# Reordering TensorE's step in a pipelined local-attention layer

## Chip, cores and metric

The kernel runs on one core of a Trainium2 chip. The metric is the device time of one launch in microseconds, lower is better. Before the change three runs gave 4150.61, 4144.84 and 4150.33 us, median 4150.33 us. A separate profiled execution took 4145.04 us.

## What is computed

The input is x, 8 sequences of 512 tokens with 128 features. Stage 1 is a causal attention with 16 heads of 8, which the change does not touch. Its output u goes through six layers of stage 2:

```
for each of 6 layers:
    xs = shift_tokens(u)                    # half of the features one token late
    q, k, v = xs @ Wqkv                     # 16 heads of 64
    q, k = rotary(l2norm(q)), rotary(l2norm(k))
    out = local_attention(q, k, v)          # windows of 32, each sees itself and the one before
    u = u + out @ Wo
    u = u + W2(a * gelu(gate)),  a, gate = W1(layernorm(shift_tokens(u)))
output = (stage 1's result) + u
```

## The kernel before, in words

Everything is laid out features by tokens. `build_stage2` (L594 on) writes one program for each engine, and the engines meet only through semaphores. Each engine executes its own list strictly in the order of the code; `wait_ge` holds the engine's queue at that place.

**The step.** A layer's attention is cut into 64 steps: 8 sequences (s) of 8 steps (p), a step being four heads of half a sequence (256 tokens). `step_no` numbers them through the program as n. The work of one step is spread over six consecutive iterations of the loop `steps` (L682), by the lags of L578: in iteration n an engine does projection and values of step n, the sum of squares and rotation of n-1 (`LAG_MIX`), the normalised queries and keys of n-2 (`LAG_NORM`), the scores of n-3 (`LAG_SCORE`), the transposes and value products of n-4 (`LAG_VALUE`) and the output projection of n-5 (`LAG_WO`). After the eighth sequence, iterations with s = 8 empty the pipeline while the feed-forward part starts. In iterations p = 6 and 7 of each sequence but the first, a layer-norm mean or variance of the previous sequence is added.

**TensorE's order in an iteration** (L1164 on):
- the mask (L1188): two bf16 products of an identity with the band, 128x256 each, put 1e30 into both score banks where a key isn't allowed; it waits for `norm_done` (queries and keys of that step written) and `exp_done` (banks read)
- the scores (L1198): 128 products of 32x32 tiles; then four transposes of the probabilities (L1178) into `tr_bank`; then mean or variance (L1150, L1154) where there is one
- the projection (L1221 to L1223): twelve fp32r products of 256 columns into `proj_ps`; it waits for `prod_done` (both rotary products of the last step have read that bank)
- the values (L1233 to L1235): three products of 512 columns into `tr_bank`, the bank that the transposes used; they wait for `pt_first` and `pt_second`, that is, until ScalarE (L907) and VectorE (L1062) have copied the transposed probabilities out
- the output projection (L1246 to L1249), six products; the value products (L1269), 32 tiles; the sums of squares (L1287).

**VectorE's order** (L1034 on): least score of both halves (L1043, `least`), copy of the transposes (L1062), `y_rest` (L1070), `centre` (L1014) at p = 6, `write_qk` (L792, two instructions that multiply `rotated` by `inv_norm`, both in SBUF), at p = 0 `divide` (L1019) and `scale_shift` (L1025), two reciprocals (L1050), at p = 4 the residual (L1092), then the cosine product (L1102) and the sine product (L1107), which read `proj_ps`.

**GpSimd's order** (L808 on): addition of the squares (L837); then, behind `prod_done`, both rotations (`rotate`, L814, SBUF only); at p = 3 the rest of the next tokens (L827); both normalisations of the probabilities (L823).

**ScalarE's order** (L893 on): at p = 3 the next tokens (L925), copy of the transposes (L907), eight exponentials (L917), the layer norm's part (L881, L886), square of the projection (L946), copy of the values out of `tr_bank` (L950), `y_high` (L958), logarithm (L967) and exponential (L973) of the sums.

SyncE's queue loads weights and tokens and moves each values tile into its shifted place (L750, L751) once `v_done` says that it is written.

## Time and profile before

| | |
|---|---|
| median of three runs | 4150.33 us |
| profiled execution | 4145.04 us |
| its span, first to last instruction | 4143.2 us |
| mean granted TensorE clock | 0.985 of full speed |
| PE busy | 3880.8 us, 94% |
| DVE busy, ACT busy, POOL busy | 76%, 76%, 61% |

PE is TensorE's matmuls and PEld its weight loads, DVE is VectorE, ACT is ScalarE, POOL is GpSimd and SP is SyncE. A row of a group gives line, engine, operation, output and inputs, shape, count, then busy time and mean ns of one, then the idle time in front of it and what ended it. A row of a timeline gives the start in us, the time in us, engine, line and operation, and merged neighbours have a count behind x. Matmuls overlap, and their ends are modelled, so the distance between two starts is what a piece of TensorE work costs.

### The profile page before, as it was taken

The page shows a single profiled execution, that of the slowest core. Times are in us where ns is not written, and L with a number is a line of the kernel's source. Part 1 is how long each engine was busy: PE and PEld are TensorE (multiplying, and loading weights), DVE is VectorE, ACT ScalarE, POOL GpSimd, SP SyncE. Part 2 cuts the span into 40 slices and gives each one's busy share as a digit, 9 for nine tenths or more (in the row PEclk, how much of TensorE's full clock was granted, in tenths as well). Part 3 has the DMA queues.
Part 4 walks back from the last instruction along what each step waited for, and adds up shares of the span by engine and source line. Part 5 has one row for each costly group of instructions (what it writes and reads, how often), then busy time and mean ns, then how long its engine had stood idle before and what let it go on. Part 6 is the DMA issues. An engine that isn't in the chain of part 4 may idle for free.

```text
span 4143.2 us, 192715 instructions
## 1 busy us (share of the span) xinstructions
PE 3880.8 (94%) x79584; PEld 3037.8 (73%) x79584; DVE 3144.8 (76%) x5678; ACT 3146.7 (76%) x10376; POOL 2543.9 (61%) x2584
## 2 busy tenths in 40 slices
PE   6888886999999999989999999999899999999998
PEld 3555554888866888848888668888488886688884
DVE  6778874888866888848888668888488886688884
ACT  5777775888865888848888658888388886588883
POOL 4766665766645666637666456666276664566660
PEclk9999998999999999999999999999999999999999
DMA  1000001111111111111111111111111111111110
GB/s 35 2 2 2 2 2 51 44 50 44 47 59 39 44 50 47 42 51 44 50 47 45 58 37 47 48 46 44 51 44 50 45 47 58 36 48 45 50 44 24
DMA packets 100984, 167.64 MB, mean 40 GB/s; under 512 B 26224, under 2 KB 33648, under 8 KB 99824
## 3 DMA queue, kind: packets, MB, share of 16 engines
q1 hardware_dynamic: 100080, 154.89, 12.7%
q8 instruction: 653, 10.70, 1.1%
q14 instruction: 251, 2.06, 0.2%
HBM read 26.13 MB, written 2.10 MB: 7 GB/s over the span
## 4 chain that ended last, share of the span: by engine, by line
PE 72%; issue 7%; POOL 3%; DVE 1%; ACT 0%; DMA 0%; SPq 0%; POOLq 0%; DVEq 0%; ACTq 0%
PE s_bank L1198 13%; PE s_bank L1269 10%; PE s_bank L1287 9%; PE s_bank L1178 6%; PE s_proj L1221 4%; PE s_proj L1222 4%; PE s_proj L1223 4%; PE s_bank L1246 2%; PE s_bank L1248 2%; PE s_bank L1249 2%; PE s_bank L1235 2%; PE s_bank L1234 2%; PE s_bank L1233 2%; PE s_bank L1188 2%; PE s_bank L1160 2%
## 5 line engine op out<-in xcount | busy, mean ns | idle before, releaser
L814 POOL TENSOR_TENSOR s_rotated<-s_rotated,s_by_sin 128x512 f32<-128x512 f32 x768 | 976.7, 1293 | 308.8 <-DVE s_by_sin L1107 308.7
L917 ACT ACTIVATE s_probs<-s_bank,s_neg_max 128x64 f32<-128x64 f32 x3072 | 900.3, 309 | 5.7 <-DVE s_neg_max L1043 5.7
L823 POOL TENSOR_TENSOR s_probs<-s_probs,s_rden 128x256 f32<-128x256 f32 x768 | 454.8, 613 | 651.1 <-DVE s_rden L1050 651.1
L1102 DVE TENSOR_TENSOR s_rotated<-s_proj,s_cos 128x1024 f32<-128x1024 f32 x384 | 469.1, 1222 | 268.1 <-ACT s_sq L946 262.6
L917 ACT ACTIVATION_READ_ACCUMULATOR s_probs<-s_bank,s_neg_max 128x1 f32 x3072 | 632.6, 206 | 0.0
L1198 PE MATMUL s_bank<-s_qk 32*32 32x64 f32 x49152 | 597.1, 224 | 10.3 <-issue 9.6
L1198 PEld LDWEIGHTS s_bank<-s_qk 32*32 32x32 f32 x49152 | 530.0, 103 | 96.8 <-issue 96.0
L792 DVE SCALAR_TENSOR_TENSOR s_qk<-s_inv_norm,s_rotated 128x512 f32<-128x512 f32 x768 | 573.5, 787 | 4.7 <-ACT s_inv_norm L973 4.5
L1221 PE MATMUL s_proj<-s_xs_high,s_w_high 128*128 128x256 f32 x1536 | 495.4, 323 | 66.6 <-POOL s_xs_rest L827 30.6
L213 POOL TENSOR_TENSOR s_probs<-s_probs,s_rden 128x384 f32<-128x384 f32 (+3 forms) x512 | 406.4, 802 | 207.6 <-DVE s_rden L406 203.8
L837 POOL TENSOR_TENSOR s_sq<-s_sq 128x512 f32<-128x512 f32 x384 | 491.8, 1281 | 59.6 <-ACT s_sq L946 59.6
L907 ACT ACTIVATE s_probs_t<-s_bank 64x512 f32<-64x512 f32 x384 | 227.1, 591 | 358.3 <-PE s_bank L1178 358.1
L1107 DVE TENSOR_TENSOR s_by_sin<-s_proj,s_sin 128x1024 f32<-128x1024 f32 x384 | 466.4, 1214 | 0.0
L946 ACT ACTIVATE s_sq<-s_proj 128x1024 f32<-128x1024 f32 x384 | 396.7, 1033 | 73.3 <-PE s_proj L1223 73.3
L1269 PE MATMUL s_bank<-s_probs_t,s_v 128*64 128x64 f32 x12288 | 451.0, 228 | 0.0
L1223 PE MATMUL s_proj<-s_xs_high,s_w_rest 128*128 128x256 f32 x1536 | 436.7, 284 | 0.0
L1222 PE MATMUL s_proj<-s_xs_rest,s_w_high 128*128 128x256 f32 x1536 | 436.1, 284 | 0.0
L1287 PE MATMUL s_bank<-s_sq,s_same_head 128*128 128x256 f32 x1536 | 435.4, 406 | 0.0
L1269 PEld LDWEIGHTS s_bank<-s_probs_t,s_v 128*64 128x64 f32 x12288 | 397.5, 140 | 51.7 <-issue 4.2
L1043 DVE TENSOR_REDUCE s_neg_max<-s_bank 128x4 f32<-128x256 f32 x768 | 291.6, 420 | 189.1 <-PE s_bank L1198 188.4
L1221 PEld LDWEIGHTS s_proj<-s_xs_high,s_w_high 128*128 128x128 f32 x1536 | 293.1, 191 | 99.9 <-issue 36.8
L295 ACT ACTIVATE s_probs<-s_bank,s_neg_max 128x384 f32<-128x384 f32 (+3 forms) x512 | 271.8, 533 | 89.4 <-DVE s_neg_max L397 85.8
(123 smaller groups left out, 8648.0 us busy)
## 6 DMA issues: line engine op xcount, KB each, us to landing
s_v<-s_v SPq DMA_DIRECT2D x384, 192.0 KB
s_v<-s_v SPq DMA_DIRECT2D x384, 64.0 KB
s_qk<-f_wqk SPq DMA_DIRECT2D x6, 1024.0 KB, 5.5
s_xs_raw<-u SPq DMA_DIRECT2D x48, 128.0 KB, 2.5
s_xf<-u SPq DMA_DIRECT2D x48, 128.0 KB, 2.4
s_xs_raw<-u SPq DMA_DIRECT2D x48, 127.8 KB, 2.8
s_xf<-u SPq DMA_DIRECT2D x48, 127.8 KB, 3.2
s_qk<-f_wv SPq DMA_DIRECT2D x6, 512.0 KB, 6.2
```

What stands on the lines that cost most here:

```text
L792: last = nc.vector.scalar_tensor_tensor(qk[:, quad % 2, i, :, at:at + TOKS], by, NORM_CUT, rotated[:, par, i, :, :], ALU.min, ALU.mult)
L814: nc.gpsimd.tensor_tensor(rotated[:, par, :, half, :], rotated[:, par, :, half, :], by_sin[:, :, 1 - half, :], (ALU.subtract, ALU.add)[half])\
L837: nc.gpsimd.tensor_tensor(own[:, :, 0, :], own[:, :, 0, :], own[:, :, 1, :], ALU.add)\
L917: last = nc.scalar.activation(probs[:, par, h, b, :], score_bank[h][:, b * KEYS:(b + 1) * KEYS], ACT.Exp, scale=-1.0, bias=neg_max[:, par, ...
L1102: nc.vector.tensor_tensor(rotated[:, par, :, :, :], proj_ps[:, :, :, :], rot_cos[:, :, :, toks], ALU.mult).then_inc(S["prod_done"], 1)
L1107: nc.vector.tensor_tensor(by_sin[:, :, :, :], proj_ps[:, :, :, :], rot_sin[:, :, :, toks], ALU.mult).then_inc(S["prod_done"], 1)
L1198: last = nc.tensor.matmul(score_bank[e][to:to + WIN, w * KEYS:(w + 1) * KEYS], qk[rows, quad % 2, 0, c, WIN + at:WIN + at + WIN], qk[rows, ...
L1221: nc.tensor.matmul(proj_ps[:, i, c, :], w[0], xs_high[:, s % 2, at:at + TOKS], start=True, stop=False)
L1222: nc.tensor.matmul(proj_ps[:, i, c, :], w[0], xs_rest[:, s % 2, at:at + TOKS], start=False, stop=False)
L1223: last = nc.tensor.matmul(proj_ps[:, i, c, :], w[1], xs_high[:, s % 2, at:at + TOKS], start=False, stop=True)
L1269: last = nc.tensor.matmul(mixed[HD * h:HD * (h + 1), pair, t, :, e, :], v[:, cols, (half * NT + t) * 2 + e, at:at + HD], probs_t[:, e, t, ...
L1287: last = nc.tensor.matmul(ss_bank[:, i * TOKS:(i + 1) * TOKS], same_head[:, :], sq[:, place(p, LAG_MIX)[2], i, 0, :], start=True, stop=True)
```

## The change

The work itself stays the same; the order on four engines, one buffer and one type change.

- TensorE, iteration n: scores (their mask is already in place), transposes, mean or variance, **output projection**, **values**, value products, sums, **projection**, **mask of the next iteration's scores**.
- The mask's operands are fp32r in place of bf16 ("rounded").
- VectorE: the second `least` goes behind the copy of the transposes. The two rotary products move to the next iteration (lag 1 in place of 0) and stand in front of `write_qk`. `y_rest` moves an iteration earlier, behind the reciprocals. `divide` and `scale_shift` go to the end.
- GpSimd: addition of squares, rest of the tokens, `rotate(0)`, both normalisations, `rotate(1)`.
- ScalarE: the values' copy and the layer norm's part go between the two halves of the exponentials; the square goes between logarithm and exponential.
- `sq` has one buffer in place of two.

```diff
@@ gpsimd
                     pool.wait_ge(S["sq_done"], m + 1)
-                    own = sq[:, place(p, LAG_MIX)[2], :, :, :]
-                    nc.gpsimd.tensor_tensor(own[:, :, 0, :], own[:, :, 0, :], own[:, :, 1, :], ALU.add)\
+                    nc.gpsimd.tensor_tensor(sq[:, :, 0, :], sq[:, :, 0, :], sq[:, :, 1, :], ALU.add)\
                       .then_inc(S["sqadd_done"], 1)
-                    pool.wait_ge(S["prod_done"], 2 * m + 2)
-                    rotate(0)
-                    rotate(1)
                 if p == XS_STEP and s < NSEQ - 1:
                     tokens_rest(s + 1)
+                if live(s, p, LAG_MIX, first):
+                    pool.wait_ge(S["prod_done"], 2 * (n - LAG_MIX) + 2)
+                    rotate(0)
                 if live(s, p, LAG_SCORE, first):
                     normalise(0)
                     normalise(1)
+                if live(s, p, LAG_MIX, first):
+                    rotate(1)
@@ scalar
                     exponentials(0)
-                if live(s, p, LAG_SCORE, first):
-                    exponentials(1)
+                if full:
+                    act.wait_ge(S["v_mm"], n + 1)
+                    nc.scalar.activation(v[:, p // TILES, 2 * (p % TILES), :], tr_bank[:, :], ACT.Copy)\
+                      .then_inc(S["v_done"], 1)
...
+                if live(s, p, LAG_SCORE, first):
+                    exponentials(1)
...
+                if full:
+                    act.wait_ge(S["proj_done"], n + 1)
+                    if not (first and p == 0):
+                        act.wait_ge(S["ss_done"], n)
+                    nc.scalar.activation(sq[:, :, :, :], proj_ps[:, :, :, :], ACT.Square)\
+                      .then_inc(S["sq_done"], 1)
@@ vector
                     least(0)
-                    least(1)
...
+                if score:
+                    least(1)
                 if ln and p == LN_STEP + 1:
                     centre(l * NSEQ + s - 1)
+                if live(s, p, LAG_MIX, first):
+
+                    m = n - LAG_MIX
+                    _, half, par = place(p, LAG_MIX)
+                    toks = slice(half * TOKS, (half + 1) * TOKS)
+                    dve.wait_ge(S["sq_done"], m + 1)
...
+                    nc.vector.tensor_tensor(rotated[:, par, :, :, :], proj_ps[:, :, :, :], rot_cos[:, :, :, toks],
+                                            ALU.mult).then_inc(S["prod_done"], 1)
...
+                    nc.vector.tensor_tensor(by_sin[:, :, :, :], proj_ps[:, :, :, :], rot_sin[:, :, :, toks],
+                                            ALU.mult).then_inc(S["prod_done"], 1)
                 if norm:
                     m = n - LAG_NORM
                     dve.wait_ge(S["inv_done"], m + 1)
...
                     write_qk(p).then_inc(S["norm_done"], 1)
@@ tensor
-                    pe.wait_ge(S["norm_done"], m + 1)
...
-                        nc.tensor.matmul(score_bank[e][:, 0:NW * KEYS], ident_b[:, :], band_b[:, 1 if half or e else 0, :],
-                                         start=True, stop=False, skip_group_check=True)
...
+                if full:
+                    if p == 0:
+                        pe.wait_ge(S["xs_rest"], l * NSEQ + s + 1)
+                    if live(s, p, LAG_VALUE, first):
+                        pe.wait_ge(S["pt_first"], n - LAG_VALUE + 1)
+                        pe.wait_ge(S["pt_second"], n - LAG_VALUE + 1)
...
...
+                if full:
+                    if not (first and p == 0):
+                        pe.wait_ge(S["prod_done"], 2 * n)
...
+                if live(s, p, LAG_SCORE - 1, first):
+
+                    half = place(p, LAG_SCORE - 1)[1]
+                    pe.wait_ge(S["norm_done"], n + 1 - LAG_SCORE + 1)
...
+                    for e in range(2):
+                        nc.tensor.matmul(score_bank[e][:, 0:NW * KEYS], ident_r[:, :], band_r[:, 1 if half or e else 0, :],
+                                         start=True, stop=False, skip_group_check=True)
```

## Rows read from the trace of the kernel before

**Rows 1.** The page's busy times of the engines.

```profile
PE 3880.8 (94%) x79584; PEld 3037.8 (73%) x79584; DVE 3144.8 (76%) x5678; ACT 3146.7 (76%) x10376; POOL 2543.9 (61%) x2584
```

**Rows 2.** Timeline of one iteration without layer norm, TensorE alone, first row of each part.

```profile
1529.03 0.65 PE L1178 MATMUL s_bank<-s_ident,s_probs 128*128 128x128 f32 x4
1529.43 0.37 PE L1221 MATMUL s_proj<-s_xs_high,s_w_high 128*128 128x256 f32 x1
...
1530.96 0.40 PE L1233 MATMUL s_bank<-s_w_high,s_xs_high 128*128 128x512 f32 x1
...
1531.66 0.28 PE L1246 MATMUL s_bank<-s_y_high,s_w_high 128*128 128x256 f32 x1
...
1532.46 1.15 PE L1269 MATMUL s_bank<-s_probs_t,s_v 128*64 128x64 f32 x32
...
1533.55 1.13 PE L1287 MATMUL s_bank<-s_sq,s_same_head 128*128 128x256 f32 x4
...
1534.51 0.38 PE L1188 MATMUL s_bank<-s_band_b,s_ident_b 128*128 128x256 bf16 x2
...
1534.82 1.56 PE L1198 MATMUL s_bank<-s_qk 32*32 32x64 f32 x128
...
1536.38 0.65 PE L1178 MATMUL s_bank<-s_ident,s_probs 128*128 128x128 f32 x4
```

**Rows 3.** The same iteration, VectorE and GpSimd.

```profile
1529.79 0.69 DVE L1062 COPY s_probs_t<-s_bank 64x512 f32<-64x512 f32 x1
...
1531.12 1.28 DVE L792 SCALAR_TENSOR_TENSOR s_qk<-s_inv_norm,s_rotated 128x512 f32<-128x512 f32 x2
...
1533.64 1.22 DVE L1102 TENSOR_TENSOR s_rotated<-s_proj,s_cos 128x1024 f32<-128x1024 f32 x1 [0.73 <-ACT s_sq L946]
...
1534.78 1.21 DVE L1107 TENSOR_TENSOR s_by_sin<-s_proj,s_sin 128x1024 f32<-128x1024 f32 x1
...
1536.08 2.52 POOL L814 TENSOR_TENSOR s_rotated<-s_rotated,s_by_sin 128x512 f32<-128x512 f32 x2 [1.09 <-DVE s_by_sin L1107]
1536.35 0.76 DVE L1043 TENSOR_REDUCE s_neg_max<-s_bank 128x4 f32<-128x256 f32 x2 [0.36 <-PE s_bank L1198]
```

**Rows 4.** Timelines, VectorE and GpSimd: first iterations of a layer; a p = 3.

```profile
3002.21 1.21 DVE L1107 TENSOR_TENSOR s_by_sin<-s_proj,s_sin 128x1024 f32<-128x1024 f32 x1
3003.34 2.38 DVE L792 SCALAR_TENSOR_TENSOR s_qk<-s_inv_norm,s_rotated 128x512 f32<-128x512 f32 x2
...
3003.50 3.35 POOL L814 TENSOR_TENSOR s_rotated<-s_rotated,s_by_sin 128x512 f32<-128x512 f32 x2 [1.12 <-DVE s_by_sin L1107]
...
849.84 2.45 DVE L792 SCALAR_TENSOR_TENSOR s_qk<-s_inv_norm,s_rotated 128x512 f32<-128x512 f32 x2
849.92 1.82 POOL L827 TENSOR_TENSOR s_xs_rest<-s_xs_raw,s_xs_high 128x544 fp32r<-128x544 f32 x1
```

**Rows 5.** Timeline of an iteration whose mask waited for `write_qk`.

```profile
3009.22 3.01 DVE L792 SCALAR_TENSOR_TENSOR s_qk<-s_inv_norm,s_rotated 128x512 f32<-128x512 f32 x2
...
3012.61 1.57 PE L1198 MATMUL s_bank<-s_qk 32*32 32x64 f32 x128
```

**Rows 6.** Groups of instructions: two weight loads and the centring.

```profile
L1221 PEld LDWEIGHTS s_proj<-s_xs_high,s_w_high 128*128 128x128 f32 x1536 | 293.1, 191 | 99.9 <-issue 36.8 <-POOL s_xs_rest L827 31.4 <-DVE s_by_sin L1107 31.0
...
L1188 PEld LDWEIGHTS s_bank<-s_band_b,s_ident_b 128*128 128x128 bf16 x768 | 73.8, 98 | 64.2 <-DVE s_qk L792 8.3 <-issue 3.4
...
L1014 DVE TENSOR_TENSOR s_xc<-s_xf,s_bank 128x512 f32<-128x512 f32 x48 | 32.6, 679 | 0.6
```

**Rows 7.** Timeline, the transposes that begin p = 0 of two sequences.

```profile
1514.32 0.65 PE L1178 MATMUL s_bank<-s_ident,s_probs 128*128 128x128 f32 x4
...
1574.77 0.65 PE L1178 MATMUL s_bank<-s_ident,s_probs 128*128 128x128 f32 x4
```

**Rows 8.** Stretches: us, busy times, PEclk (granted clock), DMA share, GB/s.

```profile
1849.00:1853.00 4.00, 3.69 (x15) 3.10 (x15) 0.00 (x0) 1.02 (x1) 0.00 (x0) 0.58 0.35 119
...
1771.00:1777.00 6.00, 4.13 (x170) 3.52 (x170) 2.50 (x6) 3.02 (x19) 1.06 (x2) 0.99 0.01 3
```

More of the change, by code:

```diff
@@ L625, in build_stage2 @@
         ident = sb("s2_ident", [P, P])
-        ident_b = sb("s2_ident_b", [P, P], BF16)
-        band_b = sb("s2_band_b", [P, 2, NW * KEYS], BF16)
+        ident_r = sb("s2_ident_r", [P, P], F32R)
+        band_r = sb("s2_band_r", [P, 2, NW * KEYS], F32R)
         same_head = sb("s2_same_head", [P, P])
@@ L639, in build_stage2 @@
         v = sb("s2_v", [P, 2, VTILES, INNER // 2])
-        sq = sb("s2_sq", [P, 2, 2, 2, TOKS])
+        sq = sb("s2_sq", [P, 2, 2, TOKS])
         by_sin = sb("s2_by_sin", [P, 2, 2, TOKS])
@@ L940, in step @@
                     log_var(f)
-                if full:
-                    act.wait_ge(S["proj_done"], n + 1)
-                    if not (first and p < 2):
-                        act.wait_ge(S["ss_done"], n - 1)
-                    nc.scalar.activation(sq[:, place(p, 0)[2], :, :, :], proj_ps[:, :, :, :], ACT.Square)\
-                      .then_inc(S["sq_done"], 1)
-                    act.wait_ge(S["v_mm"], n + 1)
-                    nc.scalar.activation(v[:, p // TILES, 2 * (p % TILES), :], tr_bank[:, :], ACT.Copy)\
-                      .then_inc(S["v_done"], 1)
+                if live(s, p, LAG_SCORE, first):
+                    exponentials(1)
                 if live(s, p, LAG_VALUE, first):
@@ L1081, in step @@
                     write_qk(p).then_inc(S["norm_done"], 1)
-                if not first and s > 1 and p == 0:
-                    divide(l, s - 2)
-                    scale_shift(l, s - 2)
                 if score:
@@ L1087, in step @@
                     inverse_sum(1)
+                if live(s, p, LAG_VALUE, first):
+                    m, par = n - LAG_VALUE, place(p, LAG_VALUE)[2]
+                    dve.wait_ge(S["y_done"], m + 1)
+                    if not (first and p == LAG_VALUE):
+                        dve.wait_ge(S["wo_done"], m)
+                    nc.vector.tensor_tensor(y_rest[:, :, :], y_bank[:, :].rearrange("p (a t) -> p a t", a=2),
+                                            y_high[:, par, :, :].bitcast(F32), ALU.subtract).then_inc(S["y_rest"], 1)
                 if not first and p == WO_STEP - 1:
@@ L1093, in step @@
                       .then_inc(S["attn_res"], 1)
-                if full:
-                    _, half, par = place(p, 0)
-                    toks = slice(half * TOKS, (half + 1) * TOKS)
-                    dve.wait_ge(S["sq_done"], n + 1)
-                    if not (first and p < 2):
-                        dve.wait_ge(S["norm_done"], n - 1)
-                    nc.vector.tensor_tensor(rotated[:, par, :, :, :], proj_ps[:, :, :, :], rot_cos[:, :, :, toks],
-                                            ALU.mult).then_inc(S["prod_done"], 1)
-                    if not (first and p == 0):
-                        dve.wait_ge(S["add_done"], 2 * n)
-                    nc.vector.tensor_tensor(by_sin[:, :, :, :], proj_ps[:, :, :, :], rot_sin[:, :, :, toks],
-                                            ALU.mult).then_inc(S["prod_done"], 1)
+                if not first and s > 1 and p == 0:
+                    divide(l, s - 2)
+                    scale_shift(l, s - 2)
             def ffn_add(f, s):
@@ L1183, in step @@
                     quad, half, par = place(p, LAG_SCORE)
-                    pe.wait_ge(S["norm_done"], m + 1)
-                    if not (first and p == LAG_SCORE):
-                        pe.wait_ge(S["exp_done"], 2 * m)
-                    for e in range(2):
-                        nc.tensor.matmul(score_bank[e][:, 0:NW * KEYS], ident_b[:, :], band_b[:, 1 if half or e else 0, :],
-                                         start=True, stop=False, skip_group_check=True)
                     for w in range(NW):
```

63 lines of the change are left out of this document (27 added, 36 removed).

## The prediction, made before the change was run

> **What bounds the kernel now.** I began with the page's busy times: PE is at 94% of the span, DVE, ACT and POOL at 76, 76 and 61% [rows 1]. A busy PE need not be a full one, so I then took the timeline of one iteration without layer norm and read distances between starts [rows 2]: transposes 0.40 us, projection 1.53, values 0.70, output projection 0.80, value products 1.09, sums 0.96, mask 0.31, scores 1.56. They add up to 7.35 us, the distance between the two transposes, 1529.03 and 1536.38. There is no hole: TensorE is the bound, and every wait of its queue has been met in time. Eight iterations from p = 0 take 1574.77 - 1514.32 = 60.45 us [rows 7], that is 1.65 more than 8 x 7.35: 0.82 for the mean and 0.82 for the variance. On the other engines [rows 3] the reader should see the cover that the order gives: between transposes and values lies the projection (1.53 us), under which the copies run; and `write_qk` (1.28 us for its two instructions) runs while GpSimd rests, its rotations having come long before.
>
> **TensorE's own work.** Nothing is added or left out, so the sum stays 7.35. The mask turns fp32r: its weight load takes 191 ns in place of 98 [rows 6], and it is now met behind a wait, where nothing hides it. Bounds: 0 (loaded ahead) and 0.09 us; its columns cost what the projection's do, about 0.12 us for 256 in both forms (1.53/12, and half of the mask's 0.31 less a change of tiles) [rows 2]. I take 0.05 us. The new wait stands in front of the scores, which is why it counts.
>
> **The values' wait.** Let T be the first transpose. Values must wait for both copies. VectorE's starts at T + 0.76 (1529.79 - 1529.03), just when the transposes are done, and takes 0.69: it ends at T + 1.45 [rows 2, 3]. TensorE now has only the six output products beside it: at the projection's pace of 0.12 us they end at T + 0.40 + 0.72 = T + 1.12. To TensorE's next product goes at least 0.05 and, with the load, some 0.20 us: values start at about T + 1.65 and 0.53 us of TensorE is lost. From there the queue runs 0.79 + 1.09 + 0.96 + 1.53, to a finished projection at T + 6.02, then mask 0.31 and scores 1.56: by TensorE's order alone an iteration would take 7.89 us.
>
> **VectorE's chain, which I expect to decide.** In the new order VectorE does between T and the mask: copy until T + 1.45, second `least` (0.76 for both, about 0.42 alone) until T + 1.90, cosine product, whose successor starts 1.14 later (T + 3.04), sine product, then `write_qk` [rows 3]. Everything is FIFO, and behind the mask's wait on `norm_done` stand the scores, behind these the transposes, behind these the copy: a closed loop with no slack. The inputs are ready: the square ends some 1.4 us before the next T. `write_qk` now starts right behind the sine product, 1.13 us after that began (T + 4.17), and in the same moment the sine product releases `rotate(0)` on GpSimd. That collision is in the trace of before, where a layer begins: sine product 3002.21, `write_qk` 3003.34, rotation 3003.50, and the two instructions take 2.38 us in place of 1.28 [rows 4]. With a single GpSimd instruction beside it, at 849.84, 2.45 us [rows 4]. So 2.38, ending at T + 6.55. From the end of `write_qk` to the first score go 0.38 us (3009.22 + 3.01 = 3012.23 to 3012.61) [rows 5], with the fp32r load 0.43. Scores start at T + 6.98, the next transposes 1.56 later: **8.55 us an iteration**, 1.20 more than now. The values' wait lies inside this loop and is not added; TensorE, done with the projection at T + 6.02, waits some 0.6 us more at the mask.
> The Trainium skill (SBUF — State Buffer, section Who interferes with whom) says that a VectorE instruction with two SBUF inputs and a GpSimd instruction that reads SBUF exclude each other for their whole length, the later one blocked. By that rule the pair would take its own 1.28 us plus a whole rotation, which by the rows is about 1.26 (half of 2.52): 2.54 us, an iteration of 8.71 us and some 4640 us in all. The row's 2.38 decides for me; that one of the two is blocked and not merely slowed fits it.
>
> **Iterations that differ.** p = 6: `centre` (0.68 us [rows 6]) joins the chain: 9.25. p = 7: the logarithm of the variance now stands behind the copy of the values, and the sums wait for it. Values start at T + 0.40 + 0.82 + 0.72 = 1.94, are in the bank at about 2.9, copy and logarithm (0.6 and 0.7, as every ScalarE pass over 512 columns) end at 4.2; sums at 4.35, so projection, mask, scores at 0.96 + 1.53 + 0.31 + 1.56 later: 8.7. p = 0: `divide` and `scale_shift` (about 1.4 us) now end VectorE's list, meet the normalisations on GpSimd, and push the next first `least`; VectorE has about 1 us spare. Cost at p = 1 between 0 and 1.1 us; I take 0.5. The residual at p = 4 (0.7 us) fits into the same spare time. SyncE's moves of the values start earlier within an iteration and are needed an iteration or more later: nothing. GpSimd: `rotate(1)` and the addition of squares end before T + 3, needed at T + 3.0 and later: nothing while a loop takes over 7 us. One buffer of `sq`: the square waits for the sums just done: nothing.
> A sequence: 8 x 8.55 + 0.7 (p = 6) + 0.15 (p = 7) + 0.5 (p = 1) = 69.75 us against 60.45 [rows 7], 9.3 more. With 7 such sequences in 6 layers: 42 x 9.3 = 391. A layer's first sequence has 5 iterations from the first score on, 1.2 each: 6 x 6 = 36. At a layer's start the values come first (0.70 us [rows 2], twice that at half clock), but the sums no longer stand behind the next values: 0. At its end the feed-forward product waits behind the mask, +1.5, and an emptier iteration follows, -0.5: 6 us. **Sum +433 us**: 4145 + 433 = 4578 for the profiled execution, whose own time is 5 us below the median of the runs; I say 4580.
>
> **Rivals.**
> 1. *No collision* (GpSimd's rotation comes late, or the pair keeps 1.28 us). Then VectorE's loop is 7.45, below the 7.89 of TensorE's order with the values' wait, which decides: (6 x 0.54 + about 0.5 + 0.6) = 4.3 us a sequence, 42 x 4.3 + 30 x 0.54 = 197, so about **4340 us**. For it: in an ordinary iteration of before no pair is slow [rows 3]. Against it: rotation and pair are now released by the same instruction. 7%.
> 2. *Faster*. The one place is the values' wait: if the copies are done before T + 1.12 (0.33 us sooner than the row says, because the first `least` no longer has the second between it and the copy), and the mask never waits, what remains is the projection's slow first product, 1.53 - 12 x 0.12 = 0.09 us an iteration, won 366 times: 4145 - 33 = **4110 us**. Against it: ScalarE, whose queue was empty, took its copy up no sooner than VectorE, so the transposes set that start. 4%.
> 3. *The clock*. TensorE now idles over 1 us an iteration. A stretch in which it was busy only 4.13 of 6 us kept 0.99 of the clock, while one that followed a long idle time had 0.58 [rows 8]. If some windows drop to 1.2 GHz, scores, mask and transposes (2.3 us of the loop) double there: one iteration in five would add 366 x 0.2 x 2.3 = 168, **4750 us**. 5%.
> 4. *The change doesn't do what it says*: the "rounded" mask falls back to a slower form of product. Sums of squares in plain f32 take 0.24 us for 256 columns (0.96/4) [rows 2], twice the 0.12; 2 x 0.12 x 366 = 88, **4670 us**. 3%.
>
> **How the numbers follow.** My forecast has 81%: both of its parts, the loop and the slow pair, stand in rows. Its unknowns are the pair (2.38 to 2.54), the load (0 to 0.09), the p = 1 delay (0 to 1.1) and gaps I have taken as zero or counted twice (0.15 us either way, 366 times, 55 us): 4490 to 4680. To that I add a little on both sides: 4470 to 4700, which also takes in rival 4; rivals 1, 2 and 3 lie outside, 16%. Faster by over 0.2% (about what a measurement can tell from no change): rival 2 alone, 4%. Within 0.2%: 1%. Slower: 95%.
>
> **What the changed kernel's profile would show.** The mean of `write_qk` (L792's successor) goes from 0.7 to about 1.2 us, its second instruction near 1.7; the mask waits for VectorE's `s_qk` in nearly all of 366 iterations, 0.5 to 0.9 us each; the values wait for the copy L1062 by about 0.5 us; T to T is 8.5 to 8.7; PE busy falls to about 85%; DVE idles only between `y_rest` and the first `least`. I am wrong if the pair stays at 1.28 us, if ScalarE or GpSimd is what TensorE waits for, if rotation and pair don't overlap, or if T to T stays under 8.

## The result, and where the profile shows it

The changed kernel took **4502.5 us** (median of 4 runs, 4497.7 to 4507.2) against 4147.6 us for the kernel before on the same chip: a ratio of 1.086 [1.084, 1.088], slower. The forecast was 4580 us in a range from 4470 to 4700; it was right in direction and range and 78 us too high. The profiled execution had a span of 4501.2 us at a mean clock of 0.99, 358 us above the span of before.

The page of the changed kernel: busy times, the chain that ended last by engine, and three groups (busy and mean ns of one, idle before and its releaser).

```profile
PE 4008.9 (89%) x79584; PEld 3062.6 (68%) x79584; DVE 3414.0 (76%) x5678; ACT 3155.0 (70%) x10376; POOL 2692.3 (60%) x2584
...
DVE 36%; PE 31%; issue 13%; POOL 2%; ACT 1%; DVEq 1%; DMA 0%; SPq 0%; POOLq 0%; ACTq 0%
...
L813 POOL TENSOR_TENSOR s_rotated<-s_rotated,s_by_sin 128x512 f32<-128x512 f32 x768 | 1135.8, 1480 | 878.2 <-DVE s_by_sin L1076 878.2
...
L791 DVE SCALAR_TENSOR_TENSOR s_qk<-s_inv_norm,s_rotated 128x512 f32<-128x512 f32 x768 | 906.5, 1221 | 0.0
...
L1286 PE MATMUL s_bank<-s_band_r,s_ident_r 128*128 128x256 f32 x768 | 188.9, 328 | 170.7 <-DVE s_qk L791 163.7
```

Two of these rows for the kernel before, the chain and the group of `write_qk`:

```profile
PE 72%; issue 7%; POOL 3%; DVE 1%; ACT 0%; DMA 0%; SPq 0%; POOLq 0%; DVEq 0%; ACTq 0%
...
L792 DVE SCALAR_TENSOR_TENSOR s_qk<-s_inv_norm,s_rotated 128x512 f32<-128x512 f32 x768 | 573.5, 787 | 4.7 <-ACT s_inv_norm L973 4.5
```

VectorE's busy time has grown by 269 us for the same 5678 instructions [rows 1], and the chain that ends last now runs through VectorE for 36% of the span, where TensorE had 72% of it. The group that grew most is `write_qk` (now L791), by 333 us: 1221 ns in the mean where it had been 787. TensorE's share of busy time fell from 94 to 89% although its instructions are the same in number, and its mask now finds `s_qk` late. The waits of the changed kernel (engine, line, waited for: us in total, times, longest us):

```profile
POOL s_rotated L813 <- DVE s_by_sin L1076: 878.2, 384, 3.5
...
PEld s_bank L1286 <- DVE s_qk L791: 239.5, 334, 2.9
...
PE s_bank L1286 <- DVE s_qk L791: 163.7, 321, 2.5
...
PEld s_bank L1224 <- ACT s_probs_t L907: 91.1, 228, 1.0
...
PE s_bank L1224 <- ACT s_probs_t L907: 52.7, 228, 0.8
...
PE s_bank L1263 <- ACT s_rstd L886: 11.6, 42, 0.3
```

The two waits that the order was expected to create are both there: the mask for `write_qk` (0.5 us each time) and the values for the copies (0.2 us each time). For the values the page names ScalarE's copy L907 as the releaser; VectorE's ends within some 0.1 us of it. The last row is the sums of squares waiting for the logarithm of the variance, and its 42 cases are the 42 iterations with p = 7. One ordinary iteration shows the loop. Timeline, start and length in us, idle time before in brackets; T, its first transpose, is 1622.44.

```profile
1622.44 0.65 PE L1173 MATMUL s_bank<-s_ident,s_probs 128*128 128x128 f32 x4
...
1623.19 0.69 DVE L1057 COPY s_probs_t<-s_bank 64x512 f32<-64x512 f32 x1 [0.36 <-PE s_bank L1173]
...
1623.92 0.42 DVE L1039 TENSOR_REDUCE s_neg_max<-s_bank 128x4 f32<-128x256 f32 x1
...
1623.99 0.47 PE L1224 MATMUL s_bank<-s_w_high,s_xs_high 128*128 128x512 f32 x1 [0.20 <-ACT s_probs_t L907]
...
1624.26 1.21 DVE L1072 TENSOR_TENSOR s_rotated<-s_proj,s_cos 128x1024 f32<-128x1024 f32 x1
...
1625.39 1.21 DVE L1076 TENSOR_TENSOR s_by_sin<-s_proj,s_sin 128x1024 f32<-128x1024 f32 x1
...
1626.52 2.38 DVE L791 SCALAR_TENSOR_TENSOR s_qk<-s_inv_norm,s_rotated 128x512 f32<-128x512 f32 x2
...
1626.68 1.67 POOL L813 TENSOR_TENSOR s_rotated<-s_rotated,s_by_sin 128x512 f32<-128x512 f32 x1 [2.40 <-DVE s_by_sin L1076]
...
1628.96 0.50 PE L1286 MATMUL s_bank<-s_band_r,s_ident_r 128*128 128x256 f32 x2 [0.47 <-DVE s_qk L791]
...
1629.39 1.48 PE L1187 MATMUL s_bank<-s_qk 32*32 32x64 f32 x128
...
1630.86 0.65 PE L1173 MATMUL s_bank<-s_ident,s_probs 128*128 128x128 f32 x4
```

The reader is to follow VectorE without a gap from the copy to 1628.90, then TensorE: mask, scores, and the transposes that release the next copy. That ring closes in 1630.86 - 1622.44 = 8.42 us, where before it was TensorE's own queue that took 7.35 [rows 2]. `write_qk` and the rotation start 0.16 us apart and take 2.38 us together, the very figure of [rows 4].

A second reading places the 358 us to within 1. For every p the distance from one iteration's first transpose to the next is taken in the trace, and its median over the 42 full sequences stands here (us; the last row is another kernel, described below):

```
kernel            p=0   p=1   p=2   p=3   p=4   p=5   p=6   p=7
before            7.34  7.32  7.34  7.33  7.32  7.32  8.11  8.11
after             8.53  8.43  8.43  8.44  8.43  8.43  9.03  8.48
rotation late     7.97  7.69  7.72  7.73  7.74  7.72  8.15  8.47
```

The rows of before and after differ by 8.01 us in a sequence, 336 us in 42. The six first sequences of a layer add 4.8 us each (29). The five stretches between the layers, 114 to 119 us in either kernel, are 7 us shorter in sum than before (577.5 for 584.6), and what follows the last layer's sequences 1 us. That makes 336 + 29 - 8 = 357 us.

### The profile page after: what moved, and what is told of

The parts are those of the page before. It is cut to its first block, busy times and chain, and to the rows that moved or that the text cites. A ratio compares the mean times of both kernels' runs of the same rounds, so it can differ in the third digit from the quotient of the medians.

```text
span 4501.2 us, 192781 instructions
## 1 busy us (share of the span) xinstructions
PE 4008.9 (89%) x79584; PEld 3062.6 (68%) x79584; DVE 3414.0 (76%) x5678; ACT 3155.0 (70%) x10376; POOL 2692.3 (60%) x2584
## 4 chain that ended last, share of the span: by engine, by line
DVE 36%; PE 31%; issue 13%; POOL 2%; ACT 1%; DVEq 1%; DMA 0%; SPq 0%; POOLq 0%; ACTq 0%
DVE s_qk L791 15%; PE s_bank L1187 12%; DVE s_rotated L1072 8%; DVE s_by_sin L1076 8%; PE s_bank L1173 6%; PE s_bank L1286 4%; DVE s_neg_max L1039 3%; PE s_bank L1155 1%; PE s_bank L1263 1%; DVE s_probs_t L1057 1%; PE s_bank L1310 1%; PE s_proj L1155 1%; PE s_bank L1149 1%; ACT s_rstd L886 1%; PE s_proj L1274 1%
## 5 line engine op out<-in xcount | busy, mean ns | idle before, releaser
L813 POOL TENSOR_TENSOR s_rotated<-s_rotated,s_by_sin 128x512 f32<-128x512 f32 x768 | 1135.8, 1480 | 878.2 <-DVE s_by_sin L1076 878.2
L917 ACT ACTIVATE s_probs<-s_bank,s_neg_max 128x64 f32<-128x64 f32 x3072 | 909.4, 311 | 2.7 <-DVE s_neg_max L1039 2.7
L791 DVE SCALAR_TENSOR_TENSOR s_qk<-s_inv_norm,s_rotated 128x512 f32<-128x512 f32 x768 | 906.5, 1221 | 0.0
L822 POOL TENSOR_TENSOR s_probs<-s_probs,s_rden 128x256 f32<-128x256 f32 x768 | 473.9, 637 | 326.5 <-DVE s_rden L1046 326.1
L1039 DVE TENSOR_REDUCE s_neg_max<-s_bank 128x4 f32<-128x256 f32 x768 | 325.1, 424 | 436.9 <-PE s_bank L1187 424.9
L907 ACT ACTIVATE s_probs_t<-s_bank 64x512 f32<-64x512 f32 x384 | 227.2, 592 | 534.8 <-PE s_bank L1173 534.8
L1187 PE MATMUL s_bank<-s_qk 32*32 32x64 f32 x49152 | 573.9, 224 | 7.4 <-issue 7.4
L1187 PEld LDWEIGHTS s_bank<-s_qk 32*32 32x32 f32 x49152 | 509.2, 103 | 67.2 <-issue 15.7
L1057 DVE COPY s_probs_t<-s_bank 64x512 f32<-64x512 f32 x384 | 266.8, 695 | 149.3 <-PE s_bank L1173 149.3
L1286 PE MATMUL s_bank<-s_band_r,s_ident_r 128*128 128x256 f32 x768 | 188.9, 328 | 170.7 <-DVE s_qk L791 163.7
```

The costliest lines, as they stand in the source:

```text
L791: last = nc.vector.scalar_tensor_tensor(qk[:, quad % 2, i, :, at:at + TOKS], by, NORM_CUT, rotated[:, par, i, :, :], ALU.min, ALU.mult)
L813: nc.gpsimd.tensor_tensor(rotated[:, par, :, half, :], rotated[:, par, :, half, :], by_sin[:, :, 1 - half, :], (ALU.subtract, ALU.add)[half])\
L822: nc.gpsimd.tensor_tensor(part, part, by, ALU.mult).then_inc(S["probs_done"], 1)
L917: last = nc.scalar.activation(probs[:, par, h, b, :], score_bank[h][:, b * KEYS:(b + 1) * KEYS], ACT.Exp, scale=-1.0, bias=neg_max[:, par, ...
L1039: nc.vector.tensor_reduce(neg_max[:, par, h, :], score_bank[h][:, 0:NW * KEYS].rearrange("p (b k) -> p b k", k=KEYS), AX, ALU.min).then_in ...
L1187: last = nc.tensor.matmul(score_bank[e][to:to + WIN, w * KEYS:(w + 1) * KEYS], qk[rows, quad % 2, 0, c, WIN + at:WIN + at + WIN], qk[rows, ...
```

## The experiments

Ratios are to the kernel before, run on the same chip in turn, with 95% intervals. "Iteration" is the median distance above, for p from 1 to 5.

### One suspected cost at a time, on the changed kernel

**The rotation taken off the pair.** GpSimd normalises first and rotates after.

```diff
-                if live(s, p, LAG_MIX, first):
-                    pool.wait_ge(S["prod_done"], 2 * (n - LAG_MIX) + 2)
-                    rotate(0)
                 if live(s, p, LAG_SCORE, first):
                     normalise(0)
                     normalise(1)
                 if live(s, p, LAG_MIX, first):
+                    pool.wait_ge(S["prod_done"], 2 * (n - LAG_MIX) + 2)
+                    rotate(0)
                     rotate(1)
```

> The changed kernel with GpSimd's first rotation behind both normalisations, so that it cannot run beside write_qk; nothing is left out. My theory (a closed loop through VectorE, 1.1 us of it the collision of write_qk with the rotation): the pair of write_qk goes from 2.38 to 1.28 us, the mask stops waiting, and an iteration falls from 8.42 to about 7.7 us, where TensorE's order with the values' wait and the projection's wait for the sine product are level. 366 x 0.72 = 264 us less than 4502: about 4240 us. Rival A (the slow pair is hidden, the values' wait alone costs the time): no change, 4490 to 4510. Rival B (only a later GpSimd matters, its normalisations now come sooner): the pair shortens but the iteration stays over 8.2.

Measured: 4283.6 us, 1.0355 [1.0338, 1.0373]. Its timeline, one iteration:

```profile
1626.78 1.22 DVE L1075 TENSOR_TENSOR s_by_sin<-s_proj,s_sin 128x1024 f32<-128x1024 f32 x1
...
1627.91 1.29 DVE L791 SCALAR_TENSOR_TENSOR s_qk<-s_inv_norm,s_rotated 128x512 f32<-128x512 f32 x2
...
1629.37 1.19 POOL L822 TENSOR_TENSOR s_probs<-s_probs,s_rden 128x256 f32<-128x256 f32 x2 [3.62 <-DVE s_rden L1045]
...
1629.72 0.39 PE L1285 MATMUL s_bank<-s_band_r,s_ident_r 128*128 128x256 f32 x2
...
1630.51 2.51 POOL L813 TENSOR_TENSOR s_rotated<-s_rotated,s_by_sin 128x512 f32<-128x512 f32 x2
```

The pair is back at 1.29 us and ends at 1629.20, half a microsecond ahead of a mask that now stands behind the projection without a wait. Three lines moved on GpSimd give back 219 us of the 358 (208 by the two ratios): the collision is the larger part of the loss. The time came out some 40 us above my figure, mostly because I had counted the gain for all 366 iterations: p = 7 gained 0.01 us (8.48 to 8.47; that alone is 30 us) and p = 0 only 0.56. The bound of p = 7 is another. Its sums wait for the logarithm of the variance in all 42 cases of this kind, in the changed kernel and in the one with both edits below, and it keeps 8.47 to 8.49 us whatever is taken from VectorE.

**VectorE's chain shortened elsewhere.** The second `least` goes back in front of the copy; the collision stays.

```diff
                 if score:
                     least(0)
+                    least(1)
                 if live(s, p, LAG_VALUE, first):
...
-                if score:
-                    least(1)
```

> The changed kernel with the second least score back in front of the copy of the transposes, where VectorE has 0.36 us to spare before the transposes are done; nothing else. If VectorE's loop (copy, least, cosine, sine, write_qk, mask, scores, transposes) sets the pace, every iteration loses the 0.38 us that this instruction holds between the copy and the cosine product: 8.42 to 8.05 us, 366 x 0.38 = 139 us, about 4363 us. If the values' wait or ScalarE's order sets it: no change, since the copy ends at the same time; 4495 to 4510.

Measured: 4403.8 us, 1.0646 [1.0628, 1.0663]; iteration 8.10 (expected 8.05), pair unchanged. TensorE has the same work and the same waits in front, so 0.33 us an iteration that appear when VectorE has one instruction fewer between the transposes and the mask show that the ring through VectorE sets the time. Again the iterations with layer norm gained less (p = 7: none), and the whole came 41 us above the figure.

**Both together.** The two edits above in one kernel.

> Both of the two: rotation behind the normalisations and the second least score in front of the copy. VectorE's loop would be near 7.0 us and the one through the projection near 7.3; what is left is TensorE's own order with the values' wait, about 7.6 us. So with the values' wait real: 4502 - 366 x 0.8 = about 4210 us, only 30 us under the run with the rotation alone, and TensorE's mask waits for nothing. If the values' wait cost nothing: iteration 7.3, about 4095 us, under the kernel before.

Measured: 4282.7 us, 1.035 [1.0332, 1.0367]; iteration 7.70 to 7.79, no shorter than that of the rotation alone. Taking 0.33 us more from VectorE bought nothing, so VectorE no longer decides. What does stands in the timeline of this kernel:

```profile
1630.88 0.65 PE L1171 MATMUL s_bank<-s_ident,s_probs 128*128 128x128 f32 x4
...
1631.95 0.28 PE L1210 MATMUL s_bank<-s_y_high,s_w_rest 128*128 128x256 f32 x1
...
1632.43 0.47 PE L1222 MATMUL s_bank<-s_w_high,s_xs_high 128*128 128x512 f32 x1 [0.21 <-ACT s_probs_t L906]
...
1635.16 0.47 PE L1272 MATMUL s_proj<-s_xs_high,s_w_high 128*128 128x256 f32 x1
```

The values start at T + 1.55 and everything behind them follows closely. The pace of the output products (0.12 us) would have let them start at 1632.07: about 0.36 us of TensorE is lost at that wait, and 7.32 + 0.36 = 7.68 is the iteration seen.

**The wait made longer.** To the kernel with both edits: the values stand in front of the output projection, directly behind the transposes.

```diff
+                if full:
...
+                    nc.tensor.matmul(tr_bank[:, :], xs_rest[:, s % 2, toks], wv[0][:, cols], start=False, stop=True)\
+                      .then_inc(S["v_mm"], 1)
                 if live(s, p, LAG_WO, first):
                     m = n - LAG_WO
...
-                if full:
...
-                    nc.tensor.matmul(tr_bank[:, :], xs_rest[:, s % 2, toks], wv[0][:, cols], start=False, stop=True)\
-                      .then_inc(S["v_mm"], 1)
```

> The run with both repairs, with the values in front of the output projection; nothing else. If an iteration of that run (7.70 us) is TensorE's own order with 0.4 us of waiting at the values, then the six output products no longer cover the copies: the values still start 1.55 us after the transposes and the 0.7 us come behind, in 282 iterations without layer norm: about 4283 + 197 = 4480 us. If something else sets the 7.70 us, less than 60 us more.

Measured: 4450.9 us, 1.0744 [1.0728, 1.0761]; iteration 8.41. The six output products were worth their own length as cover, 8.41 - 7.70 = 0.71 us (6 x 0.12 = 0.72). Timeline:

```profile
1628.73 0.65 PE L1171 MATMUL s_bank<-s_ident,s_probs 128*128 128x128 f32 x4
...
1629.48 0.59 ACT L906 ACTIVATE s_probs_t<-s_bank 64x512 f32<-64x512 f32 x1 [0.71 <-PE s_bank L1171]
1629.49 0.69 DVE L1057 COPY s_probs_t<-s_bank 64x512 f32<-64x512 f32 x1
...
1630.29 0.47 PE L1207 MATMUL s_bank<-s_w_high,s_xs_high 128*128 128x512 f32 x1 [0.91 <-ACT s_probs_t L906]
```

With these values early, no sum waits for a logarithm any more, and p = 7 takes 8.41 us like the others. Even bare, the values start at T + 1.56: the copies set that moment, and all that an order of TensorE decides is how much work lies in front of it.

**`write_qk` in front of the rotary products.** On the changed kernel, VectorE writes q and k first. A theory of the collision alone expects this to do as well as the late rotation; the ring theory expects a new ring, through the sine product that the projection waits for.

```diff
+                if norm:
+                    m = n - LAG_NORM
...
+                    write_qk(p).then_inc(S["norm_done"], 1)
                 if live(s, p, LAG_MIX, first):
...
                                             ALU.mult).then_inc(S["prod_done"], 1)
-                if norm:
-                    m = n - LAG_NORM
...
-                    write_qk(p).then_inc(S["norm_done"], 1)
```

> The changed kernel with write_qk in front of the two rotary products on VectorE; nothing else. The collision is gone here too (the rotation is released after write_qk), so whoever holds the collision alone responsible expects what the run with the late rotation gives, about 4240 us. By the loops: the sine product now ends 1.28 us later, and behind it stand the projection (1.53 us), the mask and the scores: 1.82 + 1.28 + 1.14 + 1.21 + 0.06 + 1.54 + 0.31 + 1.47 = 8.83 us an iteration, slower than the changed kernel by 0.41 x 366 = 150 us: about 4650 us, with TensorE waiting at the projection for s_by_sin and not at the mask.

Measured: 4692.6 us, 1.1346 [1.1326, 1.1366]; slower than the changed kernel by 190 us, with the pair at 1.28 us in most iterations. Its waits, and its projection in the timeline:

```profile
PEld s_proj L1274 <- DVE s_by_sin L1084: 478.7, 378, 3.6
...
PE s_proj L1274 <- DVE s_by_sin L1084: 325.3, 330, 3.2
```

```profile
1629.78 1.21 DVE L1084 TENSOR_TENSOR s_by_sin<-s_proj,s_sin 128x1024 f32<-128x1024 f32 x1
...
1631.05 0.39 PE L1274 MATMUL s_proj<-s_xs_high,s_w_high 128*128 128x256 f32 x1 [0.80 <-DVE s_by_sin L1084]
```

The projection overwrites the bank that the two products read, and now stands late in TensorE's queue: delaying its readers by 1.28 us delays it, the mask and the scores. The shortest median, at p = 2 and 5, is 8.76 (expected 8.83). At p = 3 it is 9.72: there the pair meets the tokens' rest on GpSimd and takes 2.22 us, a second collision that I had not foreseen and that makes up most of the 43 us by which the run missed my figure. In the other iterations the pair is fast and the kernel is slower all the same, so the slow pair isn't the whole of the matter; where VectorE's work lies in the ring counts too.

### The mask's form

The changed kernel with two lines edited; then the same two lines on the kernel with both edits.

```diff
-        ident_r = sb("s2_ident_r", [P, P], F32R)
-        band_r = sb("s2_band_r", [P, 2, NW * KEYS], F32R)
+        ident_r = sb("s2_ident_r", [P, P], BF16)
+        band_r = sb("s2_band_r", [P, 2, NW * KEYS], BF16)
```

> The changed kernel with the mask's two operands in bf16 again; nothing else. In the changed kernel the mask stands behind the wait for write_qk, so its weight load lies in VectorE's loop: from the end of write_qk to the first score it took 0.47 to 0.49 us with fp32r against 0.38 with bf16 in the kernel before. Expected: 366 x 0.09 = 33 us less, about 4470 us. If the load is pulled ahead of the wait: no change, 4495 to 4510.

Measured: 4467.5 us, 1.0788 [1.0769, 1.0806]; iteration 8.32, which is 0.11 less. The weight loads of the mask, in the changed kernel and in this run:

```profile
L1286 PEld LDWEIGHTS s_bank<-s_band_r,s_ident_r 128*128 128x128 f32 x768 | 115.5, 189 | 239.6 <-DVE s_qk L791 239.5
...
L1286 PEld LDWEIGHTS s_bank<-s_band_r,s_ident_r 128*128 128x128 bf16 x768 | 43.8, 97 | 242.1 <-DVE s_qk L791 239.9
```

The fp32r weight load takes 189 ns, the bf16 one 97. (The Trainium skill, TensorE: Matmul & The Clock Gate, section Weight-path perf modes, says that loads of 128 weights are fast unless the input is FP32. These two rows agree, and put fp32r with FP32.)

> The run with both repairs (rotation behind the normalisations, second least score in front of the copy), with the mask in bf16. There the mask waits for nothing and follows the projection, so its load runs beside matmuls: no change against 4283 us, within 10 us. If the type of the mask costs in itself, wherever it stands, about 30 us less as in the changed kernel.

Measured: 4280.6 us, 1.0333 [1.0315, 1.0352]: no difference that can be told from the 4282.7. The same 0.1 us costs 35 us (29 by the two ratios) where the mask is met behind a late wait and nothing where its load is done ahead.

### Parts of the change, on the kernel before

**The values in front of the projection,** TensorE's queue only.

```diff
                     if p == 0:
                         pe.wait_ge(S["xs_rest"], l * NSEQ + s + 1)
+                    if live(s, p, LAG_VALUE, first):
+                        pe.wait_ge(S["pt_first"], n - LAG_VALUE + 1)
+                        pe.wait_ge(S["pt_second"], n - LAG_VALUE + 1)
...
+                      .then_inc(S["v_mm"], 1)
+                if full:
                     if not (first and p == 0):
                         pe.wait_ge(S["prod_done"], 2 * n)
...
-                if full:
-                    if live(s, p, LAG_VALUE, first):
...
-                      .then_inc(S["v_mm"], 1)
```

> The kernel before with one edit: the values in front of the projection, that is, right behind the transposes; all else as before. This lays the wait for the copies bare: the values can start 1.55 us after the first transpose in place of 0.40. 282 iterations without layer norm lose 1.1 us, 84 with it about 0.3: 4140 + 310 + 25 = about 4475 us. If copies could be had sooner than the rows of before say: under 4300.

Measured: 4496.2 us, 1.0855 [1.0838, 1.0871]; iteration 8.38. The projection had been the cover of the values' wait, 1.53 us long against the 1.05 that the copies need behind the transposes [rows 2, 3], and the iteration has grown by 1.06. That one move costs as much as the whole change is chance: the ring that closes here is TensorE and the copies, in the changed kernel it is the one through VectorE.

**GpSimd's order only:** as in the change.

```diff
-                    pool.wait_ge(S["prod_done"], 2 * m + 2)
-                    rotate(0)
-                    rotate(1)
                 if p == XS_STEP and s < NSEQ - 1:
                     tokens_rest(s + 1)
+                if live(s, p, LAG_MIX, first):
+                    pool.wait_ge(S["prod_done"], 2 * (n - LAG_MIX) + 2)
+                    rotate(0)
                 if live(s, p, LAG_SCORE, first):
                     normalise(0)
                     normalise(1)
+                if live(s, p, LAG_MIX, first):
+                    rotate(1)
```

> The kernel before with GpSimd's part of the change alone: rest of the tokens in front of the rotations, the second rotation behind the normalisations. In this kernel the rotations run long before write_qk and an iteration is bound by TensorE, so all of it is hidden: 4142 us within 12. If GpSimd's new order costs by itself: 50 us or more.

Measured: 4182.4 us, 1.0099 [1.0083, 1.0114]: a miss, 1% where I expected none. The steps of p = 1 (8.08 for 7.32) and p = 4 (7.66 for 7.32) hold most of it; VectorE has a wait that the kernel before never met:

```profile
DVE s_by_sin L1109 <- POOL s_rotated L814: 167.0, 274, 1.4
```

The sine product reuses a buffer that the second rotation reads. With the normalisations in between, that rotation comes 1.2 us later, and behind p = 0 (`divide`, `scale_shift`) and p = 3 (the tokens' rest), where VectorE or GpSimd have more to do, the delay reaches the projection (57 waits of it for the sine product, 48.6 us; before 17, 23.2 us). I had reasoned from an ordinary iteration alone.

### Was there a faster order?

In the kernel before, TensorE changes between whole and tiled products four times an iteration. Putting the value products directly in front of the scores saves one pair of changes: sums and mask move ahead of the value products, and ScalarE's copy of their result behind the logarithm and the exponential. Edits to the kernel before, on TensorE (the moved blocks are taken out where they stood):

```diff
                     last.then_inc(S["wo_done"], 1)
+                if live(s, p, LAG_MIX, first):
...
+                    last.then_inc(S["ss_done"], 1)
+                if live(s, p, LAG_SCORE - 1, first):
+                    half = place(p, LAG_SCORE - 1)[1]
+                    pe.wait_ge(S["norm_done"], n + 1 - LAG_SCORE + 1)
...
+                        nc.tensor.matmul(score_bank[e][:, 0:NW * KEYS], ident_b[:, :], band_b[:, 1 if half or e else 0, :],
+                                         start=True, stop=False, skip_group_check=True)
                 if live(s, p, LAG_VALUE, first):
```

> A reorder of TensorE's step that lengthens no loop: the kernel before with sums and mask in front of the value products, so that these (tiles of 128x64) stand directly in front of the scores (tiles of 32x32) and TensorE changes between whole and tiled products twice an iteration in place of four times; ScalarE takes y_high behind logarithm and exponential to match. If TensorE is the bound and each change costs what the rows of before suggest (the output projection 0.80 us where six products at their pace are 0.71, the sums 0.96 where four are 0.86, the value products' end about 0.1): 0.2 to 0.25 us an iteration, 366 x 0.22 = 80 us less: about 4060 us. If the changes cost nothing or the neighbours of different tile sizes pay the same: 4142. If y_high, now later, holds ScalarE up: slower, 4200 or more.

Measured: 4331 us, 1.046 [1.0446, 1.0474], a miss. The shortest iterations did fall, to 7.1 and 7.2 us, which is the gain that I had expected, but TensorE now stopped in the middle of the scores, waiting for nothing that another engine does (timeline, TensorE):

```profile
1496.78 0.98 PE L1286 MATMUL s_bank<-s_probs_t,s_v 128*64 128x64 f32 x27
1497.69 1.07 PE L1192 MATMUL s_bank<-s_qk 32*32 32x64 f32 x75
1499.03 0.76 PE L1192 MATMUL s_bank<-s_qk 32*32 32x64 f32 x53 [0.27 <-issue]
1499.78 0.65 PE L1178 MATMUL s_bank<-s_ident,s_probs 128*128 128x128 f32 x4
```

Such gaps end 1.4 us (1.25 to 1.55) after the end of a 16384-byte transfer on the queue of kind "instruction", which itself takes 1.0 to 1.1 us: some 2.5 us from its start to the next product. In the scores every gap of over 0.25 us ends 1.2 to 1.6 us behind such a transfer, here (178) as in the two kernels below (143 and 50), although transfers are some 5 us apart. Two more runs put the supply of instructions to the test. The first has only the second block of the diff above, the mask, moved ahead of the value products, so that the sums part the two tiled runs:

> The kernel before with one edit: the mask's two products (and their wait) stand in front of the value products, the sums stay between value products and scores. The mask is thus asked for as early as in the run before this one, but no longer run of small tiled products arises (the sums part them). If the stalls of that run came from TensorE outrunning the fetch of its instructions (160 small products and 160 loads in a row), the issue waits of the scores fall back from 172 us to about 10 and the time is the kernel before's, 4145, within 20 us either way; an iteration stays at 7.3. If they came from the early mask, its wait on write_qk or its bank, the time stays near 4330 and iterations near 8.1.

Measured: 4428.9 us, 1.0677 [1.0654, 1.0701]; neither. I had missed a wait: the mask overwrites banks that ScalarE's exponentials still read.

```profile
PE s_bank L1192 <- issue: 97.7, 174, 1.7
PE s_bank L1252 <- ACT s_probs L917: 94.6, 260, 1.0
```

So a ring through the exponentials was built (its shortest iterations take 7.75), and 174 stops in the scores stayed with the sums in between, which the supply theory as I had put it did not allow. The second run has only the first block, the sums, ahead of the value products (with ScalarE's copy), and the mask where it was:

> The tiles-together run with the mask's two whole products put back between value products and scores (they take 0.3 us there), so that its order differs from the kernel before only in the sums standing ahead of the value products. In the trace of the tiles-together run, 217 of 608 transfers of 16384 bytes of instructions were followed by a stall, and TensorE went on 1.4 us after the end of each, some 2.5 us after its start; 64 value and 256 score instructions pass in 2.6 us there. If the supply of instructions is what stalls, the mask's 0.3 us lengthens that stretch to 2.9 us and most of the 172 us of issue waits at the scores go, down to some 60 or less; the time lands between 4140 and 4200. If the stalls come from the sums or ScalarE's copy of the value products standing elsewhere, they stay and the time is near 4330.

Measured: 4183.7 us, 1.0092 [1.0074, 1.0110], with both numbers inside what the supply theory gave.

```profile
PE s_bank L1198 <- issue: 46.3, 59, 1.9
```

Counted in the traces (gaps of over 0.25 us in TensorE's products that end 1.2 to 1.6 us after an instruction transfer): before 20 with 12 us, tiles together 217 with 196 us, mask early 158 with 95 us, mask back 69 with 54 us. In the last kernel the median of an ordinary iteration, 7.22 to 7.27 us, is shorter than before. It changes between whole and tiled products four times as before, so fewer changes aren't the reason, and no run shows what is. What it wins there (about 0.07 x 250 = 18 us) is less than what goes to the stops that are left and to p = 7 (8.74 for 8.11, 26 us). No order tried beat the kernel before.

## Why the prediction held, and where it was off

- **"The values' wait."** Right in kind: values at T + 1.55 (I said 1.65), because from the end of VectorE's copy to the first of them go 0.11 us (1623.88 to 1623.99) and not 0.20. The loop by TensorE's order alone was put at 7.89 and measured 7.70 where it decides; the rest of the difference lies in the scores, below. As I said, it isn't added: in the changed kernel it lies inside VectorE's ring.
- **"VectorE's chain, which I expect to decide."** Right: shortening that chain at either of two places shortened the iteration, and shortening it at both stopped paying at 7.70. The pair takes 2.38 us, 378 times of 384, its second instruction 1.78 us; with the rotation elsewhere, 1.28. Scores start at T + 6.95 (I said 6.98).
- **The size of the loop: 8.55 put, 8.43 measured.** Scores to transposes take 1.47 us here, not the 1.56 that I took from [rows 2]; the late mask isn't the reason, for the median is 1.47 to 1.49 too with the late rotation and in both runs with the values moved ahead, where the mask waits for nothing. It is 1.55 to 1.56 in the kernels whose TensorE hardly waits in an iteration (before, that with GpSimd's order only, and the last of the runs), and what makes the difference no run shows. From the pair's end to the first score go 0.49 us, for the 0.43 that I took, and the hand-overs on VectorE up to the pair are shorter by 0.09. 0.12 x 8 x 42 = 40 us.
- **"Iterations that differ."** p = 6 adds 0.60, not 0.70, and p = 7 0.05, not 0.15: 8 us. The chain that I named for p = 7 is there (the 42 waits of the sums), 8.48 us long where I put 8.7. p = 1 adds nothing, for 0.5 put; VectorE's spare time was enough, and 0.1 is found at p = 0 instead: 17 us net. This was the term with the poorest evidence, taken between bounds of 0 and 1.1.
- **Sequence and layer ends:** 29 us for the first sequences, for 36, and 8 us less at the layers' ends, where I put 6 more: 21 us. With the base of 60.45 us for eight iterations, 0.26 above the medians of before, which takes 11 us back, these add up to 40 + 8 + 17 + 21 - 11 = 75 us, the difference between the sum's 433 and the 358 measured. Nearly all these errors went the same way; their sum stayed inside the 110 us that the range allowed below the forecast.
- **TensorE's own work.** The mask's 0.05 us were 0.1 (35 us for 366 iterations and the layers' edges). This error went the other way; it is part of the 0.49 us above.
- **Rivals.** No collision: it happened, nearly always. Had it not, the time would have been 4284 and not 4340. The clock: 0.99 over the span, though TensorE waits 0.5 us at the mask and 0.2 at the values in most iterations (I had put over 1 us). Faster: no; VectorE's copy starts 0.75 us behind T, for 0.76. A slower form of mask: where its load is hidden, the kernel takes 4282.7 us with fp32r and 4280.6 with bf16, so its products aren't slower.

Most of what I expected to see in the profile was there (1221 ns, 321 mask waits of 0.5 us). T to T is 8.42, just under the 8.5 to 8.7 that I named, and the values wait 0.2 us and not 0.5. I had named VectorE's copy as what they wait for, and "ScalarE is what TensorE waits for" as a sign that I am wrong. The trace names ScalarE's copy 228 times and VectorE's 42, but both end within 0.1 us of each other and the mask's wait is the larger, so the forecast doesn't fall by it. PE's busy share is 89%, for the 85 expected, because its busy time itself has grown by 128 us. A product's record (0.28 us) is longer than its pace (0.12), so the last product in front of a wait fills a part of it, and some are recorded longer in their new places: the first output product in the mean 360 ns for 287, the mask 328 for 274, the first of the values 453 for 400.

## What to carry to other kernels

A queue that is full can be reordered only if each wait keeps as much work in front of it as the awaited engine takes: on the kernel before, moving the projection away from in front of the values' wait cost 1.06 us in an ordinary iteration, and on the kernel with both edits, where the wait was already too long for its cover, moving the output projection away cost its whole 0.71. Draw the ring through all engines for every wait that moves, see which instructions of VectorE and GpSimd it brings side by side, and read it again for the iterations that carry extra work. A cost saved outside the ring is worth nothing (the second `least`: 99 us in one kernel, 1 in the other; the bf16 mask: 35 us and 2).

## What the runs showed that I had not expected

- **VectorE and GpSimd alternate.** `write_qk`'s two instructions and one rotation, started 0.16 us apart, took 2.38 us instead of 1.28, and the rotation 1.67 instead of 1.27. If each instruction runs alone, the order is write (0.68), rotation (until 1628.35 in the timeline), write (0.55 more, until 1628.90), and the second write shows 1.78 us for 0.68. The Trainium skill (SBUF — State Buffer, section Who interferes with whom) calls it an exclusive lock held for a whole instruction; the trace agrees in kind, while its sum of whole recorded lengths, 2.54 us, is 0.16 above the measured 2.38. Recorded lengths overlap where instructions follow each other (the two writes, 0.68 long, start 0.60 apart), which would account for it.
- **The supply of instructions seems able to stop TensorE.** For it speak when the stops end and what the last run gave; the run with the early mask speaks against the simple form of it. 64 value and 256 score instructions pass in 2.6 us. With them side by side the scores waited 172 us for "issue", with two whole products of 0.3 us in between 46 us, in the old order 10 us. Why the stops stayed in the kernel whose sums part the two runs is open: its ring through the exponentials changes what TensorE has queued when a transfer starts, and no run parted the two.
